# Order of work at the starts of three blocks: first value weights, batch 1's rows in the MLP, and the head of the recurrent block

## The reference, cut to what matters

```python
x = L0(x, ctx)                  # context attention
x = L1(x, ctx)                  # channel attention
# L2, per batch:
ln = layernorm(x, ln1_s, ln1_b); q, k, v = split(ln @ w_qkv + b_qkv, 3)
x = x + merge(attention(q, k, v, ltor_mask)) @ w_ao + b_ao
x = x + merge(attention(layernorm(x) @ w_q + b_q, ctx @ w_kv + b_kv, cross_mask)) @ w_co + b_co
x = x + gelu(layernorm(x, ln3_s, ln3_b) @ w1 + b1) @ w2 + b2
# L3, per batch (a recurrent block of 32 heads of 16):
xa  = layernorm(x, ln1_w, ln1_b)
sx  = concat([state[:, 1:2] - xa[:, :1], xa[:, :-1] - xa[:, 1:]], 1)
xxx = tanh((xa + sx * maa_x) @ maa_w1)       # 5 low rank mixtures
xk, xw, xv, xr, xg = xa + sx * (maa_stack + xxx @ maa_w2)
w = exp(-exp(time_decay + tanh(xw @ td_w1) @ td_w2)); r, k, v = xr @ Wr.T, xk @ Wk.T, xv @ Wv.T
g = silu(xg @ Wg.T)
out_t = r_t . (u * k_t v_t + s_t);  s_t+1 = k_t v_t + w_t * s_t      # scan over 256 tokens
x1 = x + (groupnorm(out) * g) @ Wo.T ;  then a second mixture and a gated two layer product
```

## Time and profile before

| | |
|---|---|
| median of 3 runs | 3635.35 us (3635.02 to 3637.12) |
| the profiled execution | 3639.3 us, with a span of 3637.5 us from the first instruction to the last |
| PE busy in the span | 3411.6 us, 94% |
| DVE, POOL, ACT busy | 2321.6, 2022.3, 1821.5 us (64%, 56%, 50%) |
| mean granted clock of PE | 0.974 of full |
| token_attentions starts its first work | about 1590 us |
| token_mlp | about 2335 us |
| recurrent_block | about 2723 us |

### The profile page before, as it was taken

How to read it: one execution, slowest core, us unless ns; L and a number is a source line. 1 busy time by engine, 2 the same in 40 slices (tenths; PEclk the granted TensorE clock), 3 DMA queues, 4 the chain that set the end, 5 groups by cost and what they waited for, 6 DMA issues and landing times. The chain is left out here.

```text
span 3637.5 us, 59766 instructions
## 1 busy us (share of the span) xinstructions
PE 3411.6 (94%) x23502; PEld 2613.9 (72%) x23502; DVE 2321.6 (64%) x2874; ACT 1821.5 (50%) x4228; POOL 2022.3 (56%) x1103
## 2 busy tenths in 40 slices
PE   8989999999999999979999999699998899999978
PEld 6878778877887787657887788599985555555544
DVE  2455565566556656748777877665545678877776
ACT  2134664565456546656776776555543334343322
POOL 2235664575557556625665666455544566767753
PEclk9999999999999999989999999899998899999989
DMA  4331111121112111120002111210003000000000
GB/s 133 109 131 47 68 67 56 59 72 62 48 68 72 60 47 47 59 99 24 31 30 82 53 42 49 92 38 24 24 24 126 13 8 11 18 19 18 13 18 12
DMA packets 114302, 188.80 MB, mean 52 GB/s; under 512 B 18416, under 2 KB 36848, under 8 KB 113520
## 3 DMA queue, kind: packets, MB, share of 16 engines
q1 hardware_dynamic: 111856, 180.89, 14.8%
q10 hardware_dynamic: 2176, 4.19, 0.3%
HBM read 159.89 MB, written 25.17 MB: 51 GB/s over the span
## 5 line engine op out<-in xcount | busy, mean ns | idle before, releaser
L1030 POOL TENSOR_TENSOR l_pr<-l_pr,l_inv 128x1024 f32<-128x1024 f32 x256 | 479.7, 1894 | 383.1 <-DVE l_inv L1092 383.1
L900 ACT ACTIVATE l_pr<-l_ps_s,l_top 128x512 f32<-128x512 f32 x512 | 348.0, 689 | 352.7 <-DVE l_top L1088 275.9
L1547 POOL TENSOR_TENSOR tok_pr<-tok_pr,tok_ma 128x1024 f32<-128x1024 f32 x128 | 305.8, 2411 | 268.5 <-DVE tok_pr L1932 268.5
L2912 POOL TENSOR_TENSOR rec_rs<-rec_sE,rec_rT 128x1024 f32<-128x1024 f32 x128 | 316.7, 2474 | 231.6 <-DVE rec_sE L3423 183.3
L1025 POOL TENSOR_TENSOR l_x_lo<-ahead_piece,l_x_hi 128x1024 fp32r<-128x1024 f32 (+1 forms) x97 | 294.0, 3031 | 154.2 <-ACT l_x_hi L884 154.2
L1088 DVE TENSOR_REDUCE l_top<-l_ps_s 128x2 f32<-128x1024 f32 x256 | 304.1, 1218 | 10.5 <-PE l_ps_s L674 10.4
L3423 DVE TENSOR_TENSOR_SCAN rec_sE<-rec_wE,rec_ps_v 128x1024 f32<-128x1024 f32 x128 | 292.7, 2286 | 4.4
L684 PE MATMUL l_ps_t<-l_ident,l_pr 128*128 128x128 f32 x2048 | 275.7, 278 | 10.5 <-POOL l_pr L1030 4.5
L684 PEld LDWEIGHTS l_ps_t<-l_ident,l_pr 128*128 128x128 f32 x2048 | 225.9, 141 | 77.7 <-issue 60.7
L1807 ACT ACTIVATE tok_pr<-tok_pr,tok_shift 128x256 f32<-128x256 f32 x512 | 253.3, 497 | 10.2 <-DVE tok_shift L1940 9.6
L635 PE MATMUL l_ps_b<-l_x_hi,l_w_lo 128*128 128x256 f32 x784 | 226.7, 289 | 0.0
(11 more groups left out here) (519 smaller groups left out, 9701.0 us busy)
## 6 DMA issues: line engine op xcount, KB each, us to landing
ahead_piece<-x SPq DMA_DIRECT2D x63, 512.0 KB, 3.9
ahead_piece<-in_c SPq DMA_DIRECT2D x63, 512.0 KB, 4.8
ahead_rows<-x SPq DMA_DIRECT2D x22, 512.0 KB, 3.8
ahead_piece<-in_L_w_qk SPq DMA_DIRECT2D x16, 512.0 KB, 6.0
x<-tok_xb SPq DMA_DIRECT2D x16, 512.0 KB, 2.8
l_xt<-in_xT SPq DMA_DIRECT2D x8, 512.0 KB, 6.3
l_ct<-in_cT SPq DMA_DIRECT2D x8, 512.0 KB, 7.2
l_xn<-in_x SPq DMA_DIRECT2D x8, 512.0 KB, 4.7
```

Of the source, the lines that this page charges most:

```text
L900: act.activation(pr[t][:, h, :], ps_s[:, t % 2, h, :], ACT.Exp, bias=top[:, t, h:h + 1], accum_out=mass[:, t, h:h + 1]).then_inc(exped, 1)
L1030: pool.tensor_tensor(pr[t][:, :, :], pr[t][:, :, :], inv[:, t, :].unsqueeze(2).to_broadcast([P, 2, FEAT]), ALU.mult).then_inc(scaled, 1)
L1547: pool.tensor_tensor(tile, tile, ma[u][:, :, :].rearrange("p t k -> p (t k)").unsqueeze(1).to_broadcast([P, 2, TT * TOK]), ALU.add).then_i ...
L2912: pool.tensor_tensor(rs[j % 2][:, :, :], sE[j % 2][:, :, :], rT[s][:, :, :], ALU.mult).then_inc(rs_made, 1)
```

## The change

- Tokens: SP issues the two halves of the first value weight ahead of `open_loop`; ACT rounds it between keeping Q1 and keeping K0.
- MLP: `rows_step(0)` is 2 instead of 1; ACT does `round_hidden` ahead of `round_half` in each step. (The stages become a number with the same value, 3.)
- MLP and recurrent block: the recurrent block's columns and batch 0's edge are loaded by the MLP's SP list, after the last half, into tiles that outlast the block. SP of the recurrent block issues `m1` ahead of `open_loop` and the state tile after the small weights. ACT writes the edge column at T0. In batch 0 DVE does the subtraction for `sx` itself, in two halves as T0 and T1 are kept, and POOL doesn't. 30 instead of 52 transposes of the identity stand before XX0. In the first batch PE's step 1 is "L:G0 L:C".

```diff
 # token_attentions, SP
+            for k in range(2):
+                source = layers[0].w["QKVO".index("V")][2 * k * P:2 * (k + 1) * P, :].rearrange("(t p) n -> p t n", p=P)
+                sp.dma_start(first_v(k), source).then_inc(first_v_loaded, 16)
             open_loop(sp, loop_sems)
 # token_attentions, ACT
-                for unit in UNITS[:4]:
+                for unit in UNITS[:2]:
                     keep(1, 0, unit, 0)
                 round_first_values()
+                for unit in UNITS[2:4]:
+                    keep(1, 0, unit, 0)
 # token_mlp
     def rows_step(b):
-        return 1 if b == 0 else 0
+        return 2 if b == 0 else 0
 # token_mlp, SP, after the halves
+            sp.dma_start(ahead.cols[:, :, :], next_cols).then_inc(following.piece_loaded[0], 16)
+            sp.dma_start(ahead.edge[:, :, :], next_state[0:1, :, :, :].rearrange("o p t n -> p (o t) n")[:, :, 0:2]).then_inc(following.piece_loaded[1], 16)
 # token_mlp, ACT
                     bend(*before(b, n, 1))
+                if b or n:
+                    round_hidden(*before(b, n, 1))
                 for k in halves_in(b, n):
                     round_half(k)
-                if b or n:
-                    round_hidden(*before(b, n, 1))
 # recurrent_block
-        "L:R1 A:T0 A:T1", "L:C L:G0", "A:XX0 A:XX1", ...
+        "L:R1 A:T0 A:T1", "L:G0 L:C", "A:XX0 A:XX1", ...
 # recurrent_block, SP
+            sp.dma_start(m1[:, :, :], maa_w1.rearrange("(t p) n -> p t n", p=P)).then_inc(m1_loaded, 16)
             open_loop(sp, loop_sems)
...
-            sp.dma_start(col[:, :, :], cols).then_inc(cols_loaded, 16)
-            load_edge(0)
-            sp.dma_start(m1[:, :, :], maa_w1.rearrange("(t p) n -> p t n", p=P)).then_inc(m1_loaded, 16)
-            load_st(0, 0)
 # recurrent_block, PE
-                    keep_busy(pe, ps_acc[:, 0, 0:P], ident, 52)
+                    keep_busy(pe, ps_acc[:, 0, 0:P], ident, 30)
 # recurrent_block, DVE, unit SX
                     for c in range(FT):
+                        if b == 0 and c % 2 == 0:
+                            dve.wait_ge(keeps(b, f"T{c // 2}"), kept_by(b, f"T{c // 2}"))
+                            dve.tensor_tensor(sx[:, c:c + 2, :], xaT[:, c:c + 2, 0:TOK], xaT[:, c:c + 2, 1:TOK + 1],
+                                              ALU.subtract).then_inc(halves_shifted, 1)
+                            dve.wait_ge(halves_shifted, c // 2 + 1)
```

More of the change, by code:

```diff
@@ L2070, in weight_columns, with token_mlp @@
     return w1[:, i * FEAT:(i + 1) * FEAT].rearrange("(t p) n -> p t n", p=P)
-def token_mlp(nc, semaphores, x, w1_d, w2_d, ln_cols, b1, b2, out, ahead, here, following):
+def token_mlp(nc, semaphores, x, w1_d, w2_d, ln_cols, b1, b2, out, ahead, here, following, recurrent):
     HID = 4 * FEAT
@@ L2126, in token_mlp @@
         xb = sb("xb", [P, TT, FEAT])[:, :, :]
-        spare = sb("spare", [P, 2, FEAT])
+        spare = [sb(f"spare{i}", [P, 2, FEAT])[:, :, :] for i in range(1)]
         w2_lo = sb("w2_lo", [P, 2 * CHUNKS, FEAT], F32R)
         res = sb("res", [P, TT, FEAT])[:, :, :]
-        stages = (xb, res, spare[:, :, :])
+        stages = (xb, res, *spare)
         ps_h = [ps(f"ps_h{i}", [P, 2, TOK]) for i in range(2)]
@@ L2140, in token_mlp @@
             sem(n) for n in ("norm_loaded", "b1_loaded", "b2_loaded", "ident_made", "const_made"))
-        half_loaded = [sem(f"half_loaded{i}") for i in range(3)]
+        half_loaded = [sem(f"half_loaded{i}") for i in range(STAGES)]
         piece_hi, piece_split, half_hi, half_split = (sem(n) for n in ("piece_hi", "piece_split", "half_hi", "half_split"))
@@ L2209, in _ @@
                 load_half(k)
+            next_cols, next_state = recurrent
+            sp.dma_start(ahead.cols[:, :, :], next_cols).then_inc(following.piece_loaded[0], 16)
+            sp.dma_start(ahead.edge[:, :, :], next_state[0:1, :, :, :].rearrange("o p t n -> p (o t) n")[:, :, 0:2]).then_inc(following.piece_loaded[1], 16)
             sp.wait_ge(here.last_stored, 16)
@@ L2332, in round_half @@
             def round_half(k):
-                act.wait_ge(half_loaded[k % 3], 16 * (k // 3 + 1))
-                act.activation(half_of(k, 0), stages[k % 3], ACT.Copy).then_inc(half_hi, 1)
+                act.wait_ge(half_loaded[k % STAGES], 16 * (k // STAGES + 1))
+                act.activation(half_of(k, 0), stages[k % STAGES], ACT.Copy).then_inc(half_hi, 1)
             def evict(b, n):
@@ L2515, in recurrent_block @@
     FIRST_TENSOR_SCHEDULE = (
-        "L:R1 A:T0 A:T1", "L:C L:G0", "A:XX0 A:XX1", "L:G1", "A:Mwk0", "A:Mwk1", "A:Mvr0 A:Mvr1", "A:D1", "A:K0",
+        "L:R1 A:T0 A:T1", "L:G0 L:C", "A:XX0 A:XX1", "L:G1", "A:Mwk0", "A:Mwk1", "A:Mvr0 A:Mvr1", "A:D1", "A:K0",
         "A:K1 A:Mgd0", "A:R0 A:Mgd1", "A:R1", "A:V0", "A:V1 A:C B:T0 B:T1", "A:G0 B:XX0 B:XX1", "A:G1 B:Mwk0 B:Mwk1")
@@ L2575, in recurrent_block @@
         mean_of = sb("mean_of", [P, P])
-        NC = 16
-        col = sb("cols", [P, NC, FT])
+        col = ahead.cols
         LN1_W, LN1_B, LN2_W, LN2_B, MAA_X, DECAY0, U, GN_W, GN_B, FFN_K, FFN_R, STACK = range(12)
@@ L2586, in recurrent_block @@
         st = [sb(f"st{u}", [P, FT, 2 + GROUP]) for u in range(2)]
-        edge, a_edge = sb("edge", [P, FT, 2]), sb("a_edge", [P, FT, 2])
+        edge, a_edge = sb("edge", [P, FT, 2]), ahead.edge
         xaT, sx = sb("xaT", [P, FT, TOK + 1]), sb("sx", [P, FT, TOK])
@@ L2638, in recurrent_block @@
         shifted, mixed_x, products, mixtures, decayed, g_bent, v_hi_kept = (
[L2639 removed]
+            sem("shifted", 1, 3), sem("mixed_x", 1), sem("products", 5), sem("mixtures", 5), sem("decayed", 1), sem("g_bent", 2), sem("v_hi_kept", 2))
         spread_v, kv_made, seeded, scanned, rs_made, summed = (
@@ L2861, in a_unit @@
                                        ALU.add).then_inc(mixtures, 1)
+                elif unit == "SX" and b == 0:
+                    pool.wait_ge(mixed_x, of(b, 1, 0))
                 elif unit == "SX":
@@ L3530, in build @@
     semaphores.clear(kept)
-    token_mlp(nc, semaphores, x4, ap["L2_xattn_w1"], ap["L2_xattn_w2"], ap["L2_ln3"], ap["L2_b1"], ap["L2_b2"], x5, ahead, for_mlp, for_recurrent)
+    token_mlp(nc, semaphores, x4, ap["L2_xattn_w1"], ap["L2_xattn_w2"], ap["L2_ln3"], ap["L2_b1"], ap["L2_b2"], x5, ahead, for_mlp, for_recurrent,
+              (ap["L3_cols"], ap["L3_state"]))
     early.close()
```

26 lines of the change are left out of this document (14 added, 12 removed).

## The result

The changed kernel takes 3644.25 us (median of 10 runs, 3637.62 to 3646.54), the kernel before on the same chip 3635.05 (10 runs, 3630.53 to 3638.95): ratio 1.0025, 95% interval 1.0015 to 1.0034, that is 9.1 us slower (5.5 to 12.4). The prediction had +1.5 and a range that ended at 3641.0.

A forecast was written before the change was run, and what follows sets the result against it. PE, busy in nearly all of the span, was taken as the bound. Tokens -7.5, MLP +1.0 and +7.5, recurrent start -4.0 and gates first +4.5 gave +1.5 on 3635.35: 3636.8 us, range 3626.5 to 3641.

The forecast's parts named there:

- gates first: Recurrent block: G0 ahead of C makes batch 1's XX0 wait for DVE's keep of the shared bank; +4.5 us.
- tokens: Token block: value fills follow the keys without a wait and at full clock, less a small-columns delay; -7.5 us.
- MLP: MLP: a first wait at the turn, +1.0 us, and a new wait ahead of batch 1's hidden products, +7.5.
- recurrent, start: Start of the recurrent block: T0 no longer waits for the columns, so XX0 starts earlier; -4.0 us.
- recurrent, both: Recurrent block as a whole: earlier start, -4.0 us, together with G0 ahead of C, +4.5; predicted +0.5.
- Tokens, the last term: Token block: the moved loads delay the small columns, so ACT's first keep waits; +0.5 us (bounds 0 and 1.2).
- 5.3 us of wait at the value fills: Token block: PE's wait between keys and value fills disappears because the value weight is rounded earlier; 5.3 us gained.
- MLP, the first wait: MLP batch 0: PE still waits 10.9 us at the turn of batch 1's rows; +1.0 us (bounds 0 and +2).
- MLP, the second wait: MLP: new PE wait for the late split of batch 1's second half; 5.5 us, worked out as 4.7 to 6.2.
- gelu 0.7: MLP: duration taken for DVE's gelu product in the chain of operations after hidden 7; 0.7 us.
- The clock after the wait: MLP: PE runs at the low clock after the new wait, costing 2.0 us (bounds 0 and 2.7).
- main case: Whole kernel: all terms as summed, +1.5 us, lying in 3629 to 3641 by the bounds; chance 0.62.

The follow-up runs named there:

- a_rest: The changed kernel with its two MLP edits undone, all else kept; ratio to the kernel before 0.9990.
- r_cfirst: The changed kernel with its MLP edits undone and C ahead of G0 again in PE's step 1; ratio to the kernel before 0.9979.
- a_tokens: The kernel before with the tokens edit alone; ratio to the kernel before 0.9984.
- r_gkeep: The changed kernel with its MLP edits undone, G0 still first, DVE keeping G0 in step 1 instead of 2; ratio to the kernel before 0.9985.
- m_turnlater: The kernel before with the first half of batch 1's rows turned in the MLP's step 4 instead of 3; ratio to the kernel before 0.9985.
- m_rows2: The kernel before with `rows_step(0)` = 2 alone, order of rounding unchanged; ratio to the kernel before 1.0018.
- a_mlp: The kernel before with the two MLP edits alone (`rows_step(0)` = 2, `round_hidden` ahead of `round_half`); ratio to the kernel before 1.0028.
- m_hidfirst: The kernel before with `round_hidden` ahead of `round_half` alone, `rows_step(0)` = 1; ratio to the kernel before 1.0003.
- a_rec: The changed kernel with its tokens and MLP edits undone, leaving columns' load, recurrent start and G0 ahead of C; ratio to the kernel before 1.0008.
- m_splitearly: The changed kernel with DVE splitting the second half of batch 1's rows at the head of its step 7; ratio to the kernel before 1.0007.

## Why the prediction was wrong

The predicted mechanisms are all there, each in its place, and no rival came true. The error is in the size of the terms of the sum: every term came out on the slow side. Two things weren't in the prediction at all: the low clock in the token block's queries, and the part of gates first that comes late in the block. A slowing by over 0.2%, which is what was measured (1.0025), had been given a chance of 0.04. For an average over executions I take the table's columns: tokens 741.4 on average with the old code (six) and 737.1 with the new (six); MLP 389.1 (seven) and 400.6 (two); turn 57.3 (seven) and 55.9 (seven).

| term | predicted | block times | alone, by ratio |
|---|---|---|---|
| tokens | -7.5 | -4.3 | -5.8 |
| MLP | +8.5 | +11.5 | +10.2 |
| recurrent, start | -4.0 | -1.4 | |
| recurrent, gates first | +4.5 | +6.3 | |
| recurrent, both | +0.5 | +4.9 | +2.9 |
| sum | +1.5 | +12.1 | +7.3 |

- **Tokens, the last term.** The 5.3 us of wait at the value fills came as worked out (no gap). So did their clock (1.10 for four), but its 2.7 us are those of one execution of before: the six groups took 8.3 us in three of six with the old code and 7.0 in the other three, and take 5.6 now, a gain of about 2.0 on average. The mis-sized term is "+0.5 for the small columns": the loads' issue took 1.70 us and not 0.95, the columns behind it took 3.1 us to land and not 2.0, and the queries began 1.5 to 2.1 us late in the six executions with this edit (at 11.2 to 11.8 instead of 9.7). The low clock in the queries adds 1.1 on average (7.3 us from the first query product to the first key product, for 6.2). The predicted bounds of this term, 0 and 1.2, left all that out.
- **MLP, the first wait** (+1.0, bounds 0 and 2). PE reached `hidden(1, 0)` at 2389.20 - 2330.22 = 59.0 us after the block's start (its start at 2396.45 less the 7.25), predicted 57.2: 1.8 later. Before it was there at 56.3, so the term is +2.7 and lies outside its bounds. The turn was at 36.3, predicted 35.2.
- **MLP, the second wait** (5.5, bounds 4.7 and 6.2). It was 7.25. The failed step is "gelu 0.7": the gelu product took 1.80 beside POOL's cube, 1.1 more, and that takes the wait over its upper bound. The other part is ACT, which was 1.9 us late for the eviction of hidden 7, where 1.5 had been the worst case and about half of that was taken. 4.7 + 1.1 + 1.9 is 7.7; the other steps of the chain were some 0.4 shorter. I had taken the gelu's duration from an operation of the recurrent block, but the trace of before has both durations in the MLP's batch 0 (the cube that goes with the last row is in the earlier trace rows):

```profile
2373.57 1.29 POOL L2257 TENSOR_TENSOR ahead_piece<-ahead_piece 128x512 f32<-128x512 f32 x1 [5.64 <-DVE ahead_piece L2471]
2373.59 1.83 DVE L2463 SCALAR_TENSOR_TENSOR ahead_piece<-ahead_piece 128x512 f32<-128x512 f32 x1
...
2391.11 0.69 DVE L2463 SCALAR_TENSOR_TENSOR ahead_piece<-ahead_piece 128x512 f32<-128x512 f32 x1
```

At this place of DVE's list (2391.11) it took 0.69: DVE was busy up to it, and the product began 0.17 us ahead of POOL's cube, which then took 1.67. In the changed kernel DVE had stood idle for 0.52 us just before, and the product began 0.01 us behind the cube. That is why a duration from before would have misled here even if taken from the right row. The clock after the wait cost about what was taken (2.0): the first product took 0.58 and the next ones 0.41 each, in the earlier trace rows 0.28; 5 us at 0.55 lose 2.2. What the prediction said of the lock between DVE and POOL (the Trainium skill, "SBUF — State Buffer", section "SBUF: two separate sides") holds here: a product of two SBUF inputs that starts 0.01 behind POOL's ends 0.55 after it, 1.80 instead of 0.69. I had applied it to the split behind POOL and not to the gelu.
- **Recurrent start** (-4.0). T0 started 1.9 us after the block's start (ACT at 2732.85), as predicted, and the mixture was done after 6.2 (DVE, 2736.25 + 0.88), predicted 6.0. XX0 started at 7.0 to 8.0 instead of 6.3, since the 30 transposes held PE: they begin later than the 52 did, at the low clock, and took 4.68 here and 5.05 in a_rest. So 2.4 us were gained at XX0 in the usual execution, and of these 1.4 are left on average at the turn. That average rests on one execution: without the changed kernel's own 51.9 the new code has 56.4 to 56.8, and two of the old have 55.2 and 55.3. From XX0 to the turn the new code took 48.7 to 48.8 us in six executions of seven and 44.9 in the seventh, the old 45.0 to 48.8. By ratio the start is worth 1.8 us (r_cfirst, which is a_tokens with the new start, 0.9979 for 0.9984), within the noise. Whether an earlier start itself brings the low clock was not tested.
- **Gates first** (+4.5, bounds 2.1 and 5.0). The mechanism and the place are right to a few tenths: PE stands 8.21 us ahead of XX0 (predicted 8), DVE 4.51 ahead of step 4 (predicted 4.0, and 4.5 in all). Measured at the end it is 6.3. Scan by scan, a_rest lies 4.7 us behind r_cfirst at step 4, 3.5 at the first scan of batch 1 (the batches are counted from 0), and again more from the end of batch 3 on, in steps of 0.3 to 1.3, until 6.3. Up to there the predicted 4.5 was a fair size; what comes from batch 3 on is the part that it lacked. One such step is shown in the last section; the others weren't followed.
- **The range.** It was made of the terms' bounds, each of them read from rows of one execution. Added up plainly they reach about 3642.5, and 3641 was written. With bounds that hold what the runs showed (tokens' last term up to 2.1 and the clock 2.4 more, the first MLP wait 2.7, the second 7.4, the start -1.4, gates first 6.3) the main case would have reached 3635.35 + (-8.0 + 4.5) + (2.7 + 7.4 + 2.7) - 1.4 + 6.3, about 3650.

The view that would have helped is a timeline read for pairs: for each duration used, which operation of POOL is released together with it, which of the two starts first, and whether the change lets DVE catch up, so that the order turns round.

## What to carry to other kernels

An operation that is split off to a later step is worth following to what it then stands behind: here a cast and a subtraction behind an eviction, a gelu and a weight's split made a wait of 7 us, and putting them ahead took 6.5 back. When two products swap places on PE, their banks swap too; look for who keeps the first one, and move the keep along (r_gkeep). To give idle time to an engine move the waiting instruction alone (m_turnlater), not the whole chain that it belongs to.

## What the runs showed of the hardware

One program's executions differ in where the clock falls. With the same code up to the turn, PE's third low rank product took 1.14 us in m_rows2 and 2.08 in a_mlp and in the kernel before, and the windows there had a clock of 1.00 or of 0.50. The next two windows are of before, from 19.6 us after the block's start, and of the changed kernel, from 19.0:

```profile
2743.00:2752.00 9.00, 6.97 (x24) 3.73 (x20) 3.69 (x7) 1.68 (x4) 7.93 (x3) 0.50 1.04 390
```

```profile
2750.00:2759.00 9.00, 8.11 (x38) 6.43 (x37) 2.92 (x4) 2.66 (x8) 7.32 (x3) 1.00 1.05 390
```

Of the 7.2 us by which the changed kernel's turn came earlier in its execution (51.9 for 59.1), 3.2 were there at XX0. The other 4.0 came between XX0 and the turn, which took 44.9 us for 48.8; the old code has 45.0 there as well, in m_rows2 and m_hidfirst. Without these 4.0 us its recurrent block would have looked slower than before, which it is. One of the late steps in the loss of gates first is of this kind too: late in batch 4 both a_rest and r_cfirst have the same pause of PE, but the clock after it is up again 1.3 us later in a_rest. Windows of a_rest and of r_cfirst, at the same work:

```profile
3262.00:3264.00 2.00, 2.00 (x6) 1.56 (x6) 1.36 (x4) 0.00 (x0) 0.61 (x1) 0.50 0.00 0
3264.00:3266.00 2.00, 2.00 (x8) 1.64 (x7) 1.97 (x3) 0.00 (x0) 0.00 (x0) 0.65 0.00 0
```

```profile
3255.00:3257.00 2.00, 2.00 (x8) 1.66 (x8) 1.34 (x4) 0.00 (x0) 0.63 (x1) 0.78 0.00 0
3257.00:3259.00 2.00, 2.00 (x16) 1.30 (x14) 1.97 (x3) 0.70 (x3) 0.00 (x0) 1.00 0.00 0
```

Why it is later there is left open. a_rec and m_splitearly have their late steps at the same places as a_rest; in the changed kernel the lag behind the trace of before stays near 3.6 us until batch 6 and then grows to 5.2 and 6.0, to nearly the same total.

Which of DVE and POOL goes first is a matter of hundredths of a microsecond. In the MLP of the kernel before, 50 of the 64 gelu products began 0.01 to 0.02 us behind POOL's cube and took 1.8 us. Eleven began 0.16 ahead of it and took 0.68, and the cube then took 1.7 instead of 1.3.
